# First stage of a graph kernel: GpSimd holds the gathers of a block from tile 2 on until TensorE has transposed s of the block two back

## The reference, cut to what matters

```
neighbor = segment_sum(edge_weight[:, None] * x[src], dst)      # 53125 rows gathered from x
out0     = leaky(x @ W1.T + b1 + (neighbor + neighbor * x) @ W2.T + b2)
x1       = layernorm(x + out0 / norm(out0))
# second layer: messages x1[src] + relu(edge_attr @ ee_w1 + ee_b1) @ ee_w2 + ee_b2, summed by dst,
# then a three-layer perceptron with 1024 hidden features, layer norms, output [3125, 256]
```

## Time and profile before

| | us |
|---|---|
| median of 3 executions without a profile | 1407.51 |
| lowest and highest of them | 1405.39, 1422.13 |
| the profiled execution, its own time | 1418.96 |
| span of its trace | 1417.1 |

### The profile page before, as it was taken

How to read it: one execution, slowest core, us unless ns; L and a number is a source line. 1 busy time by engine, 2 the same in 40 slices (tenths; PEclk the granted TensorE clock), 3 DMA queues, 4 the chain that set the end, 5 groups by cost and what they waited for, 6 DMA issues and landing times.

```text
span 1417.1 us, 21215 instructions
## 1 busy us (share of the span) xinstructions
PE 1183.0 (83%) x5297; PEld 963.0 (68%) x5297; DVE 966.3 (68%) x2795; ACT 680.6 (48%) x1677; POOL 830.7 (59%) x840
## 2 busy tenths in 40 slices
PE   4787887887987778878977888998898898888897
PEld 3576666675766566666756777777776777777775
DVE  4667676685776667667866666776766666776675
ACT  2346555565565466545653344344434434533444
POOL 7566575665655656566646665665656556665530
PEclk9789898998799888998989998999999899999999
DMA  6344564555545544454666665666666566666630
GB/s 207 96 122 141 149 171 136 146 161 154 149 142 151 147 117 139 134 143 129 204 186 179 180 184 158 187 175 180 175 177 187 164 175 178 181 188 174 181 113 10
DMA packets 106088, 222.13 MB, mean 157 GB/s; under 512 B 20003, under 2 KB 57369, under 8 KB 106010
## 3 DMA queue, kind: packets, MB, share of 16 engines
q0 software_dynamic: 53408, 164.16, 41.0%
q1 hardware_dynamic: 52602, 57.11, 13.2%
HBM read 203.96 MB, written 17.23 MB: 156 GB/s over the span
## 4 chain that ended last, share of the span: by engine, by line
PE 49%; another core or an unknown queue 14%; issue 13%; DVE 12%; ACT 11%; DMA 1%; DVEq 1%; POOL 0%; ACTq 0%; POOLq 0%; SPq 0%
PE ps_z L1382 19%; PE ps_e L1104 9%; PE ps_sum L1109 5%; PE ps_sum L1111 5%; ACT aF L1884 4%; ACT msg L1654 3%; DVE msg L2158 2%; PE ps_s L1326 2%; PE ps_tr L1451 2%; PE ps_y L1382 2%; DVE msg L2164 2%; DVE oh L214 2%; ACT msg L1657 2%; PE ps_d L1186 2%
## 5 line engine op out<-in xcount | busy, mean ns | idle before, releaser
L966 POOL DMA_INDIRECT raw<-in_x,src_all x399 | 404.2, 1013 | 254.0 <-DVE msg L2164 144.8
L1027 POOL DMA_INDIRECT grow<-table_dram,src_all x401 | 390.8, 975 | 264.7 <-issue 111.7
L2158 DVE SCALAR_TENSOR_TENSOR msg<-raw,w_sb,msg 128x256 fp32r<-128x256 f32 x416 | 183.4, 480 | 208.5 <-ACT msg L1657 150.2
L1382 PE MATMUL ps_z<-w_high,a 128*128 128x512 f32 x784 | 270.0, 417 | 26.9 <-DVE a L2521 26.9
L1104 PE MATMUL ps_e<-we,attr 65*128 65x256 f32 x832 | 250.2, 425 | 44.9 <-DVE msg L2164 31.6
L1109 PE MATMUL ps_sum<-msg,oh 128*128 128x512 f32 x464 | 244.1, 526 | 9.2 <-DVE msg L2164 7.0
L1104 PEld LDWEIGHTS ps_e<-we,attr 65*128 65x128 f32 x832 | 173.1, 214 | 89.1 <-issue 59.5
L1657 ACT ACTIVATE msg<-ps_e 128x512 fp32r<-128x512 f32 (+1 forms) x220 | 123.9, 563 | 195.6 <-remote 103.2
L1382 PEld LDWEIGHTS ps_z<-w_high,a 128*128 128x128 f32 x784 | 157.1, 200 | 66.2 <-DVE a L2521 27.7
L214 DVE TENSOR_SCALAR oh<-lane,rel 128x128 fp32r<-128x128 f32 x871 | 197.8, 290 | 1.0 <-issue 0.7
L1111 PE MATMUL ps_sum<-msg,oh 128*128 128x512 f32 x464 | 195.3, 421 | 0.8 <-issue 0.8
(11 more groups left out here) (189 smaller groups left out, 1659.3 us busy)
## 6 DMA issues: line engine op xcount, KB each, us to landing
attr<-in_attrT SPq DMA_DIRECT2D x50, 192.0 KB
raw<-in_x,src_all POOLq DMA_INDIRECT x416
grow<-table_dram,src_all POOLq DMA_INDIRECT x401
w_raw<-in_m_w SPq DMA_DIRECT2D x48, 128.0 KB
table_dram<-table SPq DMA_DIRECT2D x23, 256.0 KB
attr<-in_attrT SPq DMA_DIRECT2D x24, 160.0 KB
xs<-in_x SPq DMA_DIRECT2D x24, 128.0 KB
xTb<-in_xT SPq DMA_DIRECT2D x24, 128.0 KB
```

The lines of the kernel that those rows point to most:

```text
L966: pool.indirect_dma_start(out=raw[:, j, :], out_offset=None, in_=x, in_offset=bass.IndirectOffsetOnAxis(ap=src_all[:, q * TILES + j:q * TI ...
L1027: pool.indirect_dma_start(out=grow[:, j, :].bitcast(F32), out_offset=None, in_=table_dram, in_offset=bass.IndirectOffsetOnAxis(ap=src_all[ ...
L1382: mm = pe.matmul(acc, left[a], right[b], start=False, stop=stop and a == 1, skip_group_check=True)
L2158: dve.scalar_tensor_tensor(msg[:, j, 1, 0:D], raw[:, j, :], w_sb[:, tile_cols(n, j)], msg[:, j, 0, 0:D].bitcast(F32), ALU.mult, ALU.subtract)
```

## The change

One wait is added to POOL's list. From block 4 on, before tile 2 of block q is gathered, POOL waits until s_turned has reached q-1, which is when PE has transposed s of block q-2. That happens in step 3 of block q-1. All later gathers stand behind this wait in POOL's list. In the general program, which isn't run with these inputs, nothing changes.

```diff
@@ -48,6 +48,7 @@
 LEAD = 3
+FIRST_HELD = 4
 AHEAD = 4
@@ -959,6 +960,8 @@
             def near_gathers(q):
 
                 for j in range(LAST_TILES if is_last(q) else TILES):
+                    if j == 2 and q >= FIRST_HELD:
+                        pool.wait_ge(s_turned, q - 1)
                     if j % 2 == 0:
 
                         pool.wait_ge(message, NP * (q - 1) + j // 2 + 1)
```

## The result

| us | before | after |
|---|---|---|
| median of 4 executions each, on one chip | 1413.44 | 1555.86 |
| lowest and highest | 1405.39, 1422.13 | 1549.45, 1564.16 |
| profiled execution, its own time | 1418.96 | 1561.14 |

The ratio is 1.1006, with a 95% interval of 1.095 to 1.1062: the change costs 142 us, where the prediction gave a gain of 35. Lines of the changed kernel lie one to three higher: the gathers are L969, the edge layer L1107, the transposes L1142, ACT's relu L1660 and its copy of s L1667, the message L2161 and L2167, s itself L2181.

What follows compares the result with a forecast made beforehand. Bound: a ring in which gathers delay PE's updates and so the message that stops them. 20 periods x (28.05 - 26.3) = 35 us less, from the median 1407.51 to 1372.5 us; range 1325 to 1420.

Steps and rivals of the forecast that it cites:

- What bounds the kernel: First stage: gathers hold PE's updates, these hold the message, only its absence stops the gathers; 28.05 us a block.
- The wait bites, and the transposes' update comes at once: POOL's tile 2 moves by 6.2 us in block 11; with POOL silent, ACT's 8.8 us at L1664 go.
- an update is on time up to 11.8 us after a burst has begun ... and held from 13.8 us on: Onset of the hold on PE's updates, read from the gather burst that began at 303.51.
- the burst of 286.23: Trace burst after a pause of only 2.15 us; ACT's L1664 idled 6.67 us, taken as showing short pauses don't clear long.
- T + 13.6: End of pair 4's edge layer on PE, counted from the turn T, where POOL starts its 17 gathers.
- "held" block of 28.7 us: Block whose pair 4 update is held: comes at T + 24.8, then message chain 2.9, L2178 0.42, transposes 0.60 us.
- The two follow each other: Blocks that get through (22.9 to 24.8 us) and held ones (28.7) take turns; mean of 24.8 and 28.7 is 26.8.
- The 25.9 us measured after early turns: Block period in the trace of before, over two periods after each of two turns early in a burst; supported 26.3.
- rival 2: The stall only moves, every block held at pair 4: period 28.7 or 28.05 us, 1407 to 1420 us; chance 0.19.
- Rival 4: Slower: POOL's burst meets SP's loads, gathers stretch, pair 3's edge layer is held; period 30.8, 1463 us; chance 0.14.
- 30.8 us as a bound: Longest block allowed: 28.7 plus a step of 2.13 if pair 3's update is held already; 56 us more.
- Rival 3: Late updates have nothing to do with gathers; the turn comes as late as now, about 0, 1407.5 us; chance 0.03.

Runs made afterwards that it cites:

- spacer: The changed kernel plus four short GpSimd memsets, after tiles 5, 9, 13 and 16 of each block from 4 on; 1450.31 us (before there 1412.54).
- even8: The kernel before, without the change's wait, plus an 8-column GpSimd memset after every gather from block 4 on; 1439.23 us, ratio 1.0182.

## Why the prediction was wrong

**What bounds the kernel: right.** Gathers hold PE's updates back, and the missing message is what stops the gathers. spacer and even8 show it from the other side: with the gathers spaced, no update made while they run is late.

**The wait bites, and the transposes' update comes at once: right.** ACT's copy of s is released by the transposes, POOL starts tile 2 0.8 us after their end (0.2 us was given as the sign). The forecast pause of 2 to 6 us was 11 to 15.

**The step that failed: "an update is on time up to 11.8 us after a burst has begun ... and held from 13.8 us on".** It was read from one burst. The measured onset is 4 to 5.5 us: in after, of 55 updates made in the first 4 us of a burst none was late, of 14 made in the sixth us 13 were. The burst in question has two long gathers, which the earlier trace rows leave out; the timeline of before has them:

```profile
304.77 1.61 POOL L966 DMA_INDIRECT raw<-in_x,src_all  x1 [0.30 <-issue]
...
309.26 1.54 POOL L966 DMA_INDIRECT raw<-in_x,src_all  x1 [0.30 <-issue]
```

Its first five gathers took 311.11 - 303.51 = 7.60 us, one in 1.52, which is near the rate that does no harm. Counted from 311.11, where the gathers begin to come every 1.25 us, the update of 315.32 was made 4.2 us later and came through, and that of 317.34, 6.2 us later, was held: the same onset as in after. That the long gathers put the hold off is a reading of these rows and was not tried by itself; what stretches them is open. The prediction put the late update of the burst of 286.23 down to the short pause before it, but the transposes there end at 291.61, 5.4 us into the burst, which the onset of 4 to 5.5 us covers without that. In the count over all bursts of before, 22 of 42 updates made 6 to 8 us into a burst were late already, so a look at five or six bursts would have shown it. So the update that is held is not the edge layer of pair 4 (T + 13.6) but that of pair 2, made 8.1 us into the burst.

**What that does to the sum.** The forecast's "held" block of 28.7 us had one message after the burst. Two more steps of 2.13 us make 33.0. The burst was shorter by 1.9 us (20.94 against 22.80), as it had no long gathers. The release took 3.07 us where the earlier trace rows gave 1.98. The remaining 3.0 us of the 35.2 lie in the steps after the release, among them an edge layer at half the clock after PE had idled for 6.5 us. The prediction had no term for the clock.

**"The two follow each other": wrong.** A pause of 15 us cleared the way each time, and yet each block was held, because the hold begins within the burst and needs no unclean start. The 25.9 us measured after early turns belonged to bursts that the message still broke off; the change takes just that away. The prediction saw it ("the burst is unbroken in every block, where now it is sometimes cut") and used it as a point for rival 2, without a price of its own.

**The rivals.** Rival 4 had the right condition ("updates are held less than 11.5 us after the burst's begin"), with a chance of 0.14 and a block of 30.8 us; the block was 34.7, as the update held is that of pair 2 and not of pair 3, and the steps behind it were slower. The cause that it gave was wrong: nothing stretches the gathers. The views of them from 120 to 640 us, of before and of after (shortest, median and longest in ns), have a longest of 1.24 us in after against 1.87 in before.

```profile
L966 POOL DMA_INDIRECT raw<-in_x,src_all x313: 940/947/1874, 119.8 to 634.4; - x157
```
```profile
L969 POOL DMA_INDIRECT raw<-in_x,src_all x256: 940/946/1240, 119.5 to 639.7; - x128
```

The upper end of the range, 30.8 us as a bound, was the bound of the same misread onset. Rival 3 fell with the first burst.

## What to carry to other kernels

A limit that is read from one burst is an anecdote: take the onset of a stall from all bursts in the trace, and look first at what was odd in the mildest. Where a stall is ended by the very thing that it delays, ask of a change whether it removes that brake; a wait that lets a producer fall behind and then run unbroken can cost more than the stall it cures. Make the producer wait for the signal that it holds up (here PE's sum in place of DVE's message), and the loop limits itself with no work added; here that gave 3%.

## What was not expected of the hardware

PE's semaphore updates, and of the engines counted as good as PE's alone, arrive up to 16 us late while GpSimd issues gathers one after the other, 128 rows each. A gather every 1.25 us holds them from the fourth or fifth on. With memsets between them, in the mean one in 1.62 us left next to none held, and so did one in 1.58 us in one run, but not in another; one in 1.52 us holds many. A fourfold cut of the bytes changes nothing. After the last gather of a burst the update comes 2 to 3 us later (1.98 in the earlier trace rows, 3.07 in after). A pause of 2.2 us after runs of three to six gathers clears the way, one of 1.1 us after four or five doesn't. A memset of 0.12 us between two gathers costs 0.44 us in the mean (1.69 - 1.25), most of it idle time of GpSimd behind it. By what path the gathers hold the updates is not shown by any run.
